# First attention of a graph and expert kernel: block scores, transfers that place rows, and the mean in the head weights

## The reference

```python
x_proj = layernorm(x) @ W[h]                 # 8 heads of 16 features
s = x_proj @ a_src[h];  d = x_proj @ a_dst[h]
e = leaky_relu(s[:, None] + d[None, :], 0.2) + softplus(beta) * log(prior + 1e-6)
attn = softmax(where(adj > 0, e, -inf))
x = x + concat(attn @ x_proj) @ W_out.T      # then a layernorm and the router's logits
```

## Time and profile before

| what | us |
|---|---|
| median of 3 runs | 1065.49 |
| the three runs | 1058.89, 1073.07, 1065.49 |
| span of the profiled execution | 1059.3 |
| PE busy in it | 927.0 (88%) |
| DVE busy | 717.5 (68%) |
| ACT busy | 661.1 (62%) |
| POOL busy | 504.2 (48%) |

### The profile page before, as it was taken

One profiled execution on the slowest core, in us unless ns is written; L12 is line 12 of the kernel. 1 busy time (PEld: TensorE's weight loads), 2 busy tenths in 40 slices (PEclk: granted clock), 3 DMA queues, 4 the chain that ended last, 5 costly groups with the idle time before them and its releaser, 6 DMA issues. The chain is left out here.

```text
span 1059.3 us, 25141 instructions
## 1 busy us (share of the span) xinstructions
PE 927.0 (88%) x8021; PEld 805.6 (76%) x8021; DVE 717.5 (68%) x2252; ACT 661.1 (62%) x1691; POOL 504.2 (48%) x498
## 2 busy tenths in 40 slices
PE   1799998999899999999998994798898888768997
PEld 1588887887688999999998993466565666548896
DVE  4599888988464135555554544579898888678775
ACT  4556665654544546666665662688888888867652
POOL 2566564663035564444444442576767732244340
PEclk9999998999699999999999996999999999978999
DMA  7913221211354216777676861011111100000112
GB/s 195 371 50 122 120 109 70 114 42 54 101 148 131 65 49 194 212 202 197 198 200 173 210 162 33 23 33 34 32 35 28 35 6 1 1 1 20 41 42 60
DMA packets 93007, 103.59 MB, mean 98 GB/s; under 512 B 16352, under 2 KB 69856, under 8 KB 90720
## 3 DMA queue, kind: packets, MB, share of 16 engines
q1 hardware_dynamic: 73232, 59.78, 17.3%
q10 hardware_dynamic: 11472, 25.63, 9.0%
q0 software_dynamic: 8192, 16.79, 5.5%
HBM read 52.60 MB, written 43.27 MB: 91 GB/s over the span
## 5 line engine op out<-in xcount | busy, mean ns | idle before, releaser
L1319 POOL DMA_INDIRECT slot_rows_in<-xn_all,slots x128 | 130.1, 1016 | 142.7 <-DMA slot_rows_in<-xn_all,slots 105.8
L1205 ACT ACTIVATE s_hT<-s_hp,expert 128x256 f32<-128x256 f32 x284 | 111.5, 476 | 52.4 <-PE s_hp L1196 52.4
L1218 PE MATMUL s_yp<-w_experts,s_hT 128*128 x1136 | 138.0, 275 | 0.0
L1218 PEld LDWEIGHTS s_yp<-w_experts,s_hT 128*128 128x128 f32 x1136 | 132.8, 192 | 0.0
L1226 DVE TENSOR_TENSOR xnT_all<-s_yp,expert 128x256 f32<-128x256 f32 x71 | 30.2, 425 | 117.9 <-PE s_yp L1218 114.7
L489 DVE SCALAR_TENSOR_TENSOR l_mi<-l_sbc,mT 128x512 bf16<-128x512 f32 x128 | 84.3, 668 | 4.0 <-PE l_sbc L480 3.3
L1194 PE MATMUL s_hp<-e_xh,e_wh 128*128 128x256 f32 x284 | 85.9, 303 | 0.0
L1196 PE MATMUL s_hp<-e_xh,e_wl 128*128 128x256 f32 x284 | 80.1, 282 | 0.0
L1195 PE MATMUL s_hp<-e_xl,e_wh 128*128 128x256 f32 x284 | 80.1, 282 | 0.0
L1176 ACT CAST e_wh<-expert 128x512 fp32r<-128x512 f32 x71 | 43.9, 619 | 48.8 <-issue 43.1
L1120 ACT ACTIVATE s_hT<-s_hp,b_shared 128x512 f32<-128x512 f32 x64 | 42.8, 688 | 48.4 <-PE s_hp L1091 47.2
(11 more groups left out here) (353 smaller groups left out, 2701.0 us busy)
## 6 DMA issues: line engine op xcount, KB each, us to landing
expert<-expert_rows ACTq DMA_DIRECT2D x65, 322.0 KB, 3.4
slot_rows_in<-zeros SPq DMA_DIRECT2D x9, 1024.0 KB, 12.2
xnT_all<-slot_rows_in SPq DMA_DIRECT2D x71, 128.0 KB, 3.4
slot_rows_out<-xnT_all SPq DMA_DIRECT2D x71, 128.0 KB, 2.8
slot_rows_out<-zeros SPq DMA_DIRECT2D x8, 1024.0 KB, 4.4
xn_all<-l_xr SPq DMA_DIRECT2D x16, 256.0 KB, 2.3
xnT_all<-l_rT SPq DMA_DIRECT2D x16, 256.0 KB
out_dram<-xn_all SPq DMA_DIRECT2D x16, 256.0 KB, 2.3
```

The costliest lines, as they stand in the source:

```text
L1205: nc.scalar.activation(hT[q % 2][:, c, :], hp[:, c, 0:TILE], ACT.Gelu, bias=wt[q][:, F + c:F + c + 1]).then_inc(s["h_ok"], 1)
L1218: ins = pe.matmul(yp[q % 2][:, h * D:(h + 1) * D], hT[q % 2][:, c, h * P:(h + 1) * P], w2, start=(c == 0 and h == 0), stop=(c == FC - 1), ...
L1319: pool.indirect_dma_start(k.rows_in, bass.IndirectOffsetOnAxis(ap=k.slots[:, c, b:b + 1], axis=0), k.xn[:, b, :], None).then_inc(scattered ...
```

## The change

- The scores of 4 heads in one bank come from one bf16 matmul of 512 columns over 32 rows instead of five over 128. Its weights are `dparts` (d parts where the row holds d, 1 where it holds s), its moving operand `blocks`: for head h the s parts in rows of that head, 1 in the d rows, and 0 elsewhere. The constant rows are set in setup; the s rows are placed anew for each group by eight transfers from SP, one for each head, each of 8 partitions by 256 bytes (`sp_y_blocks`). They stand on SP ahead of that group's zeroing transfer and of the keep of four groups before. The first nine zeroing transfers, issued in one go before, are now spread one a group.
- s and d are projected once (144 columns). ACT writes them twice, in fp32 and in bf16 (`sd16`); POOL subtracts for the low part (`pool_y_low`, first in its slot); PE transposes d in fp32 for the maxima, and both parts by a bf16 matmul with the identity. ACT copies this twice: to `sparts`, and with a scale and a bias per row to `dparts` (`act_y_parts`, now behind the values). DVE's maximum waits for `dparts`.
- The mean goes into the head weights: setup subtracts from `w_heads` its column means (a matmul with ones and one DVE pass), so the first normalization needs no shift. The second one's shift moves from DVE to POOL, in two passes at the end of its slot.
- The arguments of the exponentials: two DVE passes instead of four; the factors 0.2 and -0.8 go into three ACT passes of 32 columns, and the limit to at most 1 into the pass at L519.
- On ACT the high cast of the values moves ahead of `act_l_rT`, the middle cast ahead of `act_w_hT`. The slices `rows` over a whole group are what was there.
- Setup: selection matrices go; `ident16`, `is_d`, `is_s` and `blocks` are made on DVE; x's last three quarters are issued by SP, behind the weights.

```diff
             @block.sync
+                for q in range(1, 4):
+                    sp.dma_start(k.x[:, 16 * q:16 * q + 16, :],
+                                 a["x"][16 * q:16 * q + 16].rearrange("b t d -> t b d")).then_inc(k.x_loaded[q], 16)
                 sp.wait_ge(load_w, 16 * 4)
...
-                act.wait_ge(diag_made, 6)
-                nc.scalar.copy(k.sel_s[:], diag_s[:].unsqueeze(2).to_broadcast([P, HB, P]))
...
-                act.wait_ge(load_w, 16 * 4)
-                for q in range(1, 4):
-                    load_x(q)
...
+                dve.wait_ge(pool_made, 2)
+                dve.tensor_copy(k.ident16[:], k.ident[:])
+                dve.tensor_reduce(d_heads[:], k.ident[:].rearrange("p (q t c) -> p t c q", t=2, c=HEADS)[:, 1],
+                                  AX.X, ALU.max).then_inc(rows_made, 1)
...
+                chain(dve.scalar_tensor_tensor(k.w_heads[:], tr[:, 3, 0:D + 16], -1.0 / D, k.w_heads[:],
+                                               ALU.mult, ALU.add))
...
+        def act_x_scores(act, g, p):
+            wait(act, s["vs_ps"], g + 1)
+            wait(act, s["pk_ok"], g - 1)
+            nc.scalar.copy(sd[p][:].rearrange("p k b h -> p b k h"),
+                           four[:, :, D:D + 16].rearrange("p b (k h) -> p b k h", k=2)).then_inc(s["sd_ok"], 1)
+            wait(act, s["t_ps"], g)
+            nc.scalar.copy(sd16[:, :, 0, :], four[:, :, D:D + 16]).then_inc(s["s_hi"], 1)
...
+        def pool_y_low(pool, g, p):
+            wait(pool, s["sd_ok"], g + 1)
+            wait(pool, s["s_hi"], g + 1)
+            pool.tensor_tensor(sd16[:, :, 1, :].rearrange("p b (k h) -> p b k h", k=2),
+                               sd[p][:].rearrange("p k b h -> p b k h"),
+                               sd16[:, :, 0, :].rearrange("p b (k h) -> p b k h", k=2), ALU.subtract)\
+                .then_inc(s["s_lo"], 1)
...
-            pe.transpose(cc[:, 0:P], sd[p][:].rearrange("p k b h -> p (k b h)"), k.ident[:]).then_inc(s["t_ps"], 1)
+            pe.transpose(cc[0:HB, 256:256 + P], sd[p][:, 1].rearrange("p b h -> p (b h)"), k.ident[:])
+            wait(pe, s["s_lo"], g + 1)
+            pe.matmul(cc[:, 0:P], sd16[:].rearrange("p b t c -> p (b t c)"), k.ident16[:], start=True, stop=True)\
+                .then_inc(s["t_ps"], 1)
+
+        def act_y_parts(act, g, p):
             wait(act, s["t_ps"], g + 1)
+            wait(act, s["blocks_ok"], 16 * HEADS * g)
+            nc.scalar.copy(sparts[:], cc[:, 0:P]).then_inc(s["sparts_ok"], 1)
             wait(act, s["s_ps"], (g - 1) * 2 * GB)
-            nc.scalar.copy(sparts[p][:], cc[:, 0:P]).then_inc(s["hi_ok"], 1)
+            nc.scalar.activation(dparts[p][:], cc[:, 0:P], ACT.Identity, scale=k.is_d[:], bias=k.is_s[:])\
+                .then_inc(s["dparts_ok"], 1)
+
+        def sp_y_blocks(sp, g, p):
+            wait(sp, s["sparts_ok"], g + 1)
+            wait(sp, s["s_ps"], (g - 1) * 2 * GB)
+            for h in range(HEADS):
+                sp.dma_start(k.blocks[p][h:P:16, h, :], sparts[h:P:16, :]).then_inc(s["blocks_ok"], 16)
...
         def dve_y_max(dve, g, p):
-            wait(dve, s["hi_ok"], g + 1)
+            wait(dve, s["dparts_ok"], g + 1)
...
-            dve.tensor_scalar(pk[p][:, 1], pk[p][:, 0], 0.2, None, ALU.mult)
-            dve.tensor_scalar(pk[p][:, 2], us[:], -0.8, 0.0, ALU.mult, ALU.min).then_inc(s["pk_ok"], 1)
+            dve.tensor_tensor(pk[p][:, 1], cc[:, P:P + HB], s_i, ALU.add).then_inc(s["pk_ok"], 1)
...
-            nc.scalar.activation(bdg[p][:], pk[p][:], ACT.Exp).then_inc(s["bdg_ok"], 1)
+            nc.scalar.activation(bdg[p][:, 0], pk[p][:, 0], ACT.Exp)
+            nc.scalar.activation(bdg[p][:, 1], pk[p][:, 0], ACT.Exp, scale=0.2).then_inc(s["bdg_ok"], 1)
+            nc.scalar.activation(bdg[p][:, 2], pk[p][:, 1], ACT.Exp, scale=-0.8).then_inc(s["row_exp"], 1)
...
         def pe_z_scores(pe, g, p, b):
             if b == 0:
-                wait(pe, s["sp_ok"], g + 1)
+                wait(pe, s["blocks_ok"], 16 * HEADS * (g + 1))
+                wait(pe, s["dparts_ok"], g + 1)
+            rows = slice(32 * b, 32 * b + 32)
             for h in range(2):
                 wait(pe, s["mi_ok"], g * 2 * GB + 2 * b + h - 1)
-                c = b * HEADS + 4 * h
-                pe.matmul(sbc[:, h, :].rearrange("p (q i) -> p q i", q=4), sparts[p][:], k.sel_d[:, c:c + 4, :],
-                          start=True, stop=False, skip_group_check=True)
-                for q in range(4):
-                    ins = pe.matmul(sbc[:, h, q * P:(q + 1) * P], k.sel_s[:, c + q, :], sparts[p][:],
-                                    start=False, stop=(q == 3), skip_group_check=True)
-                ins.then_inc(s["s_ps"], 1)
+                pe.matmul(sbc[:, h, :].rearrange("p (q i) -> p q i", q=4), dparts[p][rows, :],
+                          k.blocks[p][rows, 4 * h:4 * h + 4, :], start=True, stop=True).then_inc(s["s_ps"], 1)
...
-            if on["r"]:
-                dve_r_shift(dve, g - 2)
-            if on["n"]:
-                dve_x_shift(dve, g + 3, q)
...
                 act_x_scores(act, g + 1, q)
-                act_y_hi(act, g + 1, q)
                 act_x_values(act, g + 1, q)
+                act_y_parts(act, g + 1, q)
...
             if on["x"]:
                 act_x_xT(act, g + 2, p)
+            if on["y"]:
+                act_y_vhi(act, g + 1, q)
             if on["l"]:
                 act_l_rT(act, g - 3)
-            if on["y"]:
-                act_y_vhi(act, g + 1, q)
...
                 act_x_rstd(act, g + 3, q)
+            if on["y"]:
+                act_y_vmid(act, g + 1, q)
             if on["w"]:
                 act_w_hT(act, g - 1, q)
-            if on["y"]:
-                act_y_vmid(act, g + 1, q)
...
+            if on["y"]:
+                pool_y_low(pool, g + 1, q)
             if on["w"]:
                 pool_z_post(pool, g - 1, q, 3)
...
                 pool_z_post(pool, g, p, 2)
+            if on["r"]:
+                pool_r_shift(pool, g - 2)
...
+                for g in range(GROUPS + 4):
+                    if g < GROUPS:
+                        sp_y_blocks(sp, g, g % 2)
+                    zero_piece(g)
+                    if g >= 4:
+                        sp_keep(sp, g - 4)
```

More of the change, by code:

```diff
@@ L254, in _ @@
                 pe.transpose(tr[:, 1, 0:P], u_ij[:], k.ident[:]).then_inc(pe_t, 1)
+                pe.wait_ge(ones_made, 1)
+                pe.wait_ge(dve_s, 17)
+                pe.matmul(tr[:, 3, 0:D + 16], k.ones[:], k.w_heads[:], start=True, stop=True).then_inc(pe_t, 1)
 def head_attention_phase(nc, k, a):
@@ L296, in head_attention_phase @@
         heads = [sb(f"l0_heads{b}", [P, HEADS, VW]) for b in range(2)]
-        shift = [sb(f"l0_shift{p}", [P, GB]) for p in range(2)]
         act_fence, act_fence_r = sb("l0_act_fence", [P, 1]), sb("l0_act_fence_r", [P, 1])
@@ L330, in dve_x_stats @@
                     dve.wait_ge(k.x_loaded[g // 4], 16)
+            wait(dve, s["var"], g)
             for b in range(GB):
@@ L333, in dve_x_stats @@
             ins.then_inc(s["stats"], 1)
+            wait(dve, s["lnv_done"], g - 1)
             wait(dve, s["stats"], g + 1)
@@ L344, in act_x_rstd @@
             nc.scalar.activation(rstd[p][:], lnv[:], ACT.Exp, scale=-0.5).then_inc(s["rstd_ok"], 1)
-        def dve_x_shift(dve, g, p):
-            wait(dve, s["xn_ok"], g - 1)
-            wait(dve, s["rstd_ok"], g + 1)
-            dve.scalar_tensor_tensor(shift[p][:], mv[p][:, :, 0], -1.0, rstd[p][:], ALU.mult, ALU.mult)\
-                .then_inc(s["shift_ok"], 1)
         def act_x_apply(act, g, p):
             wait(act, s["xT_ps"], g)
-            wait(act, s["shift_ok"], g + 1)
-            nc.scalar.copy(act_fence[:], shift[p][:, 0:1])
+            wait(act, s["rstd_ok"], g + 1)
+            nc.scalar.copy(act_fence[:], rstd[p][:, 0:1])
             for b in range(GB):
                 ins = nc.scalar.activation(xn[:, b:b + 1, :], k.x[:, bass.ds(g * GB + b, 1), :], ACT.Identity,
-                                           scale=rstd[p][:, b:b + 1], bias=shift[p][:, b:b + 1])
+                                           scale=rstd[p][:, b:b + 1])
             ins.then_inc(s["xn_ok"], 1)
@@ L424, in pe_y_maxima @@
             wait(pe, s["diag_ok"], g + 1)
-            pe.matmul(cc[:, P:P + HB], k.ones[32:64, :], dmdiag[32:64, :], start=True, stop=True)\
+            pe.matmul(cc[:, P:P + HB], k.ones[0:HB, :], dmdiag[0:HB, :], start=True, stop=True)\
                 .then_inc(s["dm_ps"], 1)
@@ L429, in dve_y_small @@
             wait(dve, s["dm_ps"], g + 1)
[L430 removed]
+            wait(dve, s["row_exp"], g - 1)
             s_i = sd[p][:, 0].rearrange("p b h -> p (b h)")
@@ L452, in act_y_vhi @@
+            pool.tensor_tensor(vp[:, rows, VW:2 * VW], k.v17[p][:, rows, :],
+                               bdg[p][:, 1, rows].unsqueeze(2).to_broadcast([P, HB, VW]), ALU.mult)\
+                .then_inc(s["vp_ok"], 1)
```

(12 more changed lines are left out.)

134 lines of the change are left out of this document (57 added, 77 removed).

## The result

| | median us | lowest to highest | runs |
|---|---|---|---|
| before | 1063.83 | 1058.89 to 1073.07 | 4 |
| after | 1105.75 | 1100.94 to 1109.29 | 4 |

The ratio is 1.0373 (95% interval 1.0298 to 1.0448): slower by 41.9 us, against a forecast of 6.4 faster. Each ratio compares an experiment with runs of before on the same chip, whose medians were 1073.82, 1061.53 and 1072.49 us on the three chips used. Slots, marks and granted clocks are each read from one profiled execution.

A forecast was written before the change was run, and what follows sets the result against it. TensorE and VectorE shared the bound before; a closed loop was to set the new slot. Slots -2.3, low clock +2.4, start -5.0, end -1.5 sum to -6.4: from the median 1065.5 to 1059 us, range 1034 to 1078.

The forecast's parts named there:

- the low clock: PE in the first attention: 1.2 GHz level in half of eleven slots, costing 1.3 us in two of them, +2.4 us.
- the loop: First attention: value chain, hT, projection, scores, maxima and back form a closed ring that sets the slot at 14.11 us.
- The clock stays low: Rival, chance 0.1: PE's 3.75 us in the ring takes up to twice as long, +2.5 in all 15 slots, 1096.5 us.
- -2.3: First attention's slots: four early ones of 13.2 us and eleven of 14.11, 208.0 against 210.3 us.
- The scores: PE, one block's score matmuls: 0.44 us instead of 0.87, with ends 0.2 and 0.6; 1.7 us less a slot.
- The stalls: VectorE's four-column shift passes held up by GpSimd passes: all 14.1 us, 0.94 a slot, would go.
- The biased copy: ScalarE's second copy, with scale and bias, before VectorE's maximum: takes 0.48 us, ends 0.3 to 0.7.
- The start: Setup: x's issues moved to SP let the next block begin at 13.8 instead of 18.80, -5.0 us.
- The transfers: SP's eight transfers per group: 0.67 us an issue, 2.3 to land, first there at 34.3, just in time.
- The end: After the last value chain: scores up to 1.7 us less, the moved shift adds 0.3 in two slots, -1.5.

The follow-up runs named there:

- `rows128`: Changed kernel with each score matmul over all 128 rows instead of its batch's 32, so sums run over four batches: 1076.47 us, 0.998 of before.
- `before32`: Kernel before with its five score matmuls over 32 rows instead of 128, nothing else of the change: 1108.19 us, ratio 1.0445.
- `fill`: Changed kernel plus 16 unread full-row identity matmuls in PE's idle gap ahead of the maxima: 1100.4 us, ratio 1.0261.
- `shifts`: Kernel before with the mean in the head weights, the first shift gone, the second moved from VectorE to GpSimd: 1063.75 us, ratio 0.9957.
- `shifts_start`: `shifts` with x's last three quarters issued by SP behind the weights: 1059.03 us, 0.9888 of before.
- `full`: Changed kernel with score weights zero-padded to 128 rows, one copy per batch filled by four ScalarE passes, results unchanged: 1064.27 us, ratio 1.0038.
- `full_order`: `full` with ScalarE's old order, high cast behind the copy of rT and middle cast behind hT: 1063.83 us, ratio 1.0021.
- `order`: Changed kernel with ScalarE's old order, high cast behind the copy of rT and middle cast behind hT: 1108.92 us, ratio 1.0326.

## Why the prediction was wrong

**The step that failed: the low clock.** I expected it "in half of the eleven slots; PE work outside the loop has 1.4 us to spare", +2.4 us. It came in every slot of the steady part, for 10 to 14 us at a time, and then PE itself was the bound (18.93 of 20 us busy), so that nothing was left to spare. After ends the phase 320.66 - 278.04 = 42.6 us behind the same kernel over 128 rows: 36.7 in slots, 5.7 behind them, 0.2 ahead. The rival "The clock stays low", at a chance of 0.1, gave +2.5 a slot and 1096.5 us; 2.45 and 1105.75 were measured. Its size was right and its reason was not, and the match is in part luck: it let 3.75 us of PE work in a closed loop take longer, while in after the loop is open and all of PE's work counts. I argued for and against it from gaps, "PE is idle 1.4 us before the projection and 0.9 before the maxima", and `rows128` has such gaps in every slot at a clock of 0.97. What I read past is in the diff: `rows` makes the form 32*128.

The Trainium skill's account (TensorE: Matmul & The Clock Gate, HAM oscillation), which I named beside this rival, tells of a PE whose wait for a transfer is longer than its burst of matmuls. I read it too widely: by it this rival was not the likely one, since PE has no such wait in these slots, and it does not explain the loss, since PE was busy 18.93 of 20 us in after and the clock of `before32` fell with 0.18 us of idle time in 6.

**The loop: right at the full clock.** `rows128` is the nearest to the forecast's kernel in timing. Its eleven steady slots have a median of 14.06 us, forecast 14.11; their mean is 14.28, for one of 16.15. The four early ones have 13.29, forecast 13.2. PE's projection waits for hT there as foreseen:

```profile
L570 PE MATMUL l_yy<-w_outT,l_hT 128*128 128x128 f32 x128 | 19.4, 297 | 18.7 <-ACT l_hT L564 18.7
```

18.7 us, 1.2 in each of 16 slots, against 1.4 forecast and 1.5 in all before. In after the same group waits 1.9 in all: a slow PE is late for everything, and the loop opens. The measured 14.02 of `rows128` is also before's slot to the last digit, so over 128 rows the gain in the slots is nothing: the stalls go and the loop takes their place. `rows128` has three short stretches at the low clock in these slots, so it is to be held against -2.3 and +2.4 together, +0.1: right.

**The scores.** Forecast 0.44 a block. At the full clock one takes 0.43 over 128 rows (in `rows128`, 156.25 to 156.68), but 0.53 over 32, as the changed kernel has it (166.14 to 166.67 above) and `fill` again and again; over 64 rows it is 0.53 too. So the cut in rows made the block dearer by 0.10 even where the clock was full. That is inside the forecast's ends of 0.2 and 0.6, and of the 42.6 us it is at most 6.4 for 64 blocks (an estimate: 64 times 0.10).

**The stalls.** All gone, as the rule on the shared port said (the Trainium skill, SBUF — State Buffer, Who interferes with whom): no VectorE pass of four columns is left that could stall. The trace agrees: L350 took 2.25 us beside a GpSimd pass of 2.25, and on GpSimd the two passes of the shift take 0.20 each.

**The biased copy.** Forecast 0.48; 0.47 in after (L410). PE's idle time before the maxima is 1.07 in the slot shown, and 0.6 to 1.2 in those of `rows128`; forecast 0.9.

**The start.** Forecast -5.0; the block starts 3.5 earlier (15.3 against 18.80) and the first cast 4.0. Both SP and VectorE were late, in after:

```profile
4.23 10.40 SPq L136 DMA_DIRECT2D x_tok<-in_x_dram  x3
15.26 3.21 SPq L798 DMA_DIRECT2D w_fc<-in_L_gnn_W_fc_dram  x1
```

```profile
11.79 0.43 DVE L221 TENSOR_TENSOR wa_prod<-w_heads,a_heads 128x256 f32<-128x256 f32 x1 [2.04 <-DMA a_heads<-in_L_gnn_a_dst_dram]
```

SP's three issues of x take 10.40 us and end at 14.63; I had put them there and given them no cost. VectorE waits 2.04 us for `a_heads`, issued at 3.31 just ahead of x, and its setup ends at 14.45. So of all engines SP ends last, and the block starts 0.6 behind it, as it started 0.7 behind ScalarE's last issue before. That x's transfers delay `a_heads` is shown by `shifts` and `shifts_start`, which differ in who issues x and when; PE's first matmul waits for it:

```profile
9.51 0.44 PE L254 MATMUL setup_tr<-ident,w_out_in 128*128 128x128 f32 x1 [9.51 <-DMA a_heads<-in_L_gnn_a_dst_dram]
```

```profile
11.67 0.45 PE L256 MATMUL setup_tr<-ident,w_out_in 128*128 128x128 f32 x1 [11.67 <-DMA a_heads<-in_L_gnn_a_dst_dram]
```

**The transfers.** Eight issues take 4.85 us, 0.6 each, under the 0.67 forecast, and PE waits for them in the first slot only:

```profile
134.62 4.85 SPq L417 DMA_DIRECT2D blocks<-l_sparts  x8
```

```profile
33.59 1.03 PE L489 MATMUL l_sbc<-blocks,l_dparts 32*128 32x512 bf16 x2 [3.80 <-DMA blocks<-l_sparts]
```

The last landed at about 33.6, forecast 34.3. PE had little else to do in that first slot: the second cast came 12.4 us after the first (23.9 and 36.3) where I had estimated 12.0, so by that estimate the wait of 3.80 cost 0.4.

**The end.** Forecast -1.5; from last cast to mark `rows128` takes 44.1 against 40.7: +3.4. The pairs `full` and `full_order` (44.5, 40.2) and after and `order` (49.8, 42.7) put most of it on the order of the casts, by one trace each. From 248 to 256 the granted clock is 0.50 in `full` and 1.00 in `full_order`; why it falls just there stays open.

For the phase as a whole, with the scores over 128 rows: forecast -6.4, measured 278.04 - 278.83 = -0.8. Of the 5.6 us between them 4.9 are at the end and 0.8 at the start. So even without the low clock's loss the change would have gained next to nothing.

## What to carry to other kernels

Cutting a matmul's rows to those that hold data saved no time here (0.53 us a block against 0.43 over all rows), and it cost the clock of everything around it: when an edit changes the number before the star in a matmul's form, ask for the granted clock and not for the duration. Zeros in the unused rows of the weights are a cheap cure: they are set once, and what remains is to write each group's data into its own block, here four passes for one; place those passes where their engine waits, not ahead of a copy that PE needs. A gap next to a fall of the clock is not yet its cause: a kernel with the same gap and another form tells. And an order of casts is to be read together with what stands between them: here a pass that waited for statistics (L339) held both.

## What the hardware showed that I had not expected

The granted clock stayed at 0.50 with PE busy 4.00 of 4.00 us, and at 1.00 with PE busy 2.89 of 4.00. Rows in use ordered the kernels (0.70, 0.86 and 0.97 at 32, 64 and 128), and zero weights counted as use (0.99 over 60 to 220 in `full`). In after each fall came at an idle gap, and in `before32` two came with 0.18 us of idle time in 6, so gaps help to set the moment and the rows decide whether it falls and how soon it returns. It is not a level that every slot meets alike: `rows128` has a window of 0.62 at 160 to 164, and `fill` swings between both levels. A block of two score matmuls took 0.53 us over 32 or 64 rows and 0.43 over 128, at the full clock; why is open. At which mixture of matmuls the clock lets go was not measured.
